# Query and key norms of a gated delta layer: the keys' read off a diagonal, the queries' summed in 32-column tiles

## The reference, cut to what matters

```python
q, k, v = split(silu(causal_conv(hidden @ w_qkv, conv_w)))       # heads of 128
qf = q * rsqrt(sum(q * q) + 1e-6) * 128 ** -0.5
kf = k * rsqrt(sum(k * k) + 1e-6)
def step(state, xs):                                             # over the tokens
    state = state * exp(g_t)
    delta = (v_t - k_t @ state) * b_t
    state = state + outer(k_t, delta)
    out = q_t @ state
```

## Time and profile before

| | |
|---|---|
| median of three runs | 1787.74 us (1787.28 to 1789.94) |
| the profiled execution | 1803.65 us, span 1802.1 us |
| TensorE matmuls | 1571.8 us busy, 87% of the span |
| VectorE | 1033.7 us, 57% |
| ScalarE | 771.8 us, 43% |
| GpSimd | 800.1 us, 44% |
| key and query norms (L593) | 512 passes, 60.5 us |
| k_root (L1056) | 16, mean 1638 ns |
| loads of A0, issue to landing | 2.6 us, median |

### The profile page before, as it was taken

One profiled execution on the slowest core, in us unless ns is written; L12 is line 12 of the kernel. 1 busy time (PEld: TensorE's weight loads), 2 busy tenths in 40 slices (PEclk: granted clock), 3 DMA queues, 4 the chain that ended last, 5 costly groups with the idle time before them and its releaser, 6 DMA issues. The chain is left out here.

```text
span 1802.1 us, 27445 instructions
## 1 busy us (share of the span) xinstructions
PE 1571.8 (87%) x9790; PEld 1149.2 (64%) x9790; DVE 1033.7 (57%) x2127; ACT 771.8 (43%) x1745; POOL 800.1 (44%) x1336
## 2 busy tenths in 40 slices
PE   3749999999999999999999999986979995978860
PEld 2436777777777777777778778764547764635540
DVE  4426677677777777777777777553035555312323
ACT  1325565565565565565565655541124331100110
POOL 0367667656656756757657657100000000061326
PEclk9779999999999999999999999998989996789995
DMA  4111111111111111111111111004210001023424
GB/s 154 38 27 26 32 38 28 36 33 30 39 33 30 34 33 36 33 33 36 34 33 37 33 33 23 8 10 197 112 30 1 1 1 53 1 85 86 144 86 116
DMA packets 119087, 84.41 MB, mean 47 GB/s; under 512 B 92658, under 2 KB 104518, under 8 KB 118192
## 3 DMA queue, kind: packets, MB, share of 16 engines
q1 hardware_dynamic: 112304, 64.73, 13.1%
q0 software_dynamic: 6656, 18.01, 3.3%
HBM read 63.00 MB, written 20.05 MB: 46 GB/s over the span
## 5 line engine op out<-in xcount | busy, mean ns | idle before, releaser
L580 PE MATMUL psum_banks<-main_hT,heads_w_in 128*128 128x512 f32 x512 | 248.7, 612 | 19.1 <-DVE heads_y L882 11.0
L882 DVE SCALAR_TENSOR_TENSOR heads_y<-psum_banks,gdn_conv_w,heads_y 128x1021 f32<-128x1021 f32 (+2 forms) x192 | 244.7, 1275 | 28.4 <-ACT heads_y L756 27.4
L1069 POOL TENSOR_TENSOR heads_XT<-heads_XT,heads_tmp 128x126 f32<-128x126 f32 (+22 forms) x496 | 207.1, 418 | 38.9
L1066 POOL TENSOR_TENSOR heads_tmp<-heads_XT,heads_A 128x126 f32<-128x126 f32 (+22 forms) x496 | 184.0, 371 | 38.9
L1604 POOL DMA_INDIRECT expert_rows<-moe_xn,route_dest x32 | 31.4, 981 | 365.5 <-issue 365.5
L580 PEld LDWEIGHTS psum_banks<-main_hT,heads_w_in 128*128 128x128 f32 x512 | 93.9, 196 | 94.8 <-issue 69.4
L667 PE MATMUL psum_banks<-heads_w_z,main_hT 128*128 128x256 f32 x512 | 126.6, 392 | 0.0
L693 PE MATMUL psum_banks<-heads_w_o,heads_ogT 128*128 128x256 f32 x512 | 119.2, 381 | 2.9 <-ACT heads_ogT L818 1.0
L756 ACT ACTIVATE heads_y<-psum_banks,gdn_conv_w 128x1024 f32<-128x1024 f32 x64 | 71.3, 1114 | 114.2 <-PE psum_banks L580 114.2
L778 ACT ACTIVATE heads_Dt<-heads_Dl,gdn_coef 128x128 f32<-128x128 f32 x224 | 77.4, 393 | 90.7 <-DVE heads_Dl L895 89.3
L1053 POOL TENSOR_TENSOR heads_Dm<-heads_Dm,main_upto 128x512 f32<-128x512 f32 x64 | 87.0, 1380 | 52.8 <-ACT heads_Dm L816 52.8
(11 more groups left out here) (249 smaller groups left out, 3511.0 us busy)
## 6 DMA issues: line engine op xcount, KB each, us to landing
main_w_gu<-in_w_gu SPq DMA_DIRECT2D x4, 2816.0 KB, 24.9
heads_w_in<-in_w_in SPq DMA_DIRECT2D x16, 512.0 KB
heads_A<-kk_blocks SPq DMA_DIRECT2D x64, 128.0 KB, 2.6
moe_wd<-in_w_down POOLq DMA_DIRECT2D x32, 176.0 KB, 2.7
expert_rows<-main_zeros SPq DMA_DIRECT2D x1, 4096.0 KB, 14.5
heads_w_z<-in_w_z SPq DMA_DIRECT2D x16, 256.0 KB, 2.7
heads_w_o<-in_w_o SPq DMA_DIRECT2D x16, 256.0 KB, 2.7
inverse_blocks<-heads_XT SPq DMA_DIRECT2D x32, 128.0 KB, 2.9
```

What stands on the lines that cost most here:

```text
L580: ins = pe.matmul(out[:, half * 512:(half + 1) * 512], w_in[:, kd_, j * P:(j + 1) * P], hT[:, kd_, half * 512:(half + 1) * 512], start=kd_ ...
L882: dve.scalar_tensor_tensor(y[j][:, shift:T], src[:, 0:T - shift], conv_w[:, head, j, t:t + 1], y[j][:, shift:T], ALU.mult, ALU.add).then_i ...
L1066: pool.tensor_tensor(tmp[:, 0:n, 0:m], bc_last(XT[:, 0:n, j], m), bc_mid(A0[:, j, j + 1:BLK], n), ALU.mult).then_inc(solve_step.sem, 1)
L1069: pool.tensor_tensor(XT[:, 0:n, j + 1:BLK], XT[:, 0:n, j + 1:BLK], tmp[:, 0:n, 0:m], ALU.add).then_inc(solve_step.sem, 1)
```

## The change

The products for the key norms, the squares of the keys and their PSUM bank's slot go. `block_scales` now also turns `nd`, which holds the squared norms (plus 1e-6) block by block, on VectorE in four squares of 32 x 32, and copies from it, quadrant by quadrant, to `k_norm`; GpSimd takes `k_root` inside `eliminate`, behind the scaling of A0. The query norms stay on TensorE, with the operands' places exchanged: the stationary operand is 32 columns of ones, and the squares are streamed, block b of all chunks (256 columns) to the partitions 32b to 32b+31. All 32 rows of such a block are equal, so VectorE turns the result from PSUM to `q_rows` and takes every 32nd column.

```diff
-    [("norm_k", 1), ("u6a", 3), ("u6b", 0)],
+    [("u6a", 3), ("u6b", 0)],
...
-AT = {"variance": 3, "factors": 6, "turn": 8, "scales": 13, "keys": 5, "key_squares": 8}
+AT = {"variance": 3, "factors": 6, "turn": 8, "scales": 13, "keys": 5}
...
+    q_rows = a.sb("q_rows", [P, C, BLK])
-    ones_col = a.sb("ones_col", [P, 1])
+    ones_col = a.sb("ones_col", [P, BLK])
+    nd_t = a.sb("nd_t", [P, BLK])
...
             def norms(out, squares):
-                for c in range(C):
-                    ins = pe.matmul(out[:, c:c + 1], squares[:, c * P:(c + 1) * P], ones_col[:], start=True, stop=True)
+                tokens = squares[:].rearrange("p (c b i) -> p b c i", b=NB, i=BLK)
+                for b in range(NB):
+                    ins = pe.matmul(out[BLK * b:BLK * (b + 1), 0:C * BLK], ones_col[:], tokens[:, b], start=True, stop=True)
                 return ins
...
-            pe.wait_ge(k_ready.sem, 2)
             pe.wait_ge(s_const, 1)
-            pe.wait_ge(s_first_kneg, 1)
-            norms(pair[:, 0:P], y[0]).then_inc(s_first_norm, 1)
...
-            key_squares(0, 1)
...
                 dve.tensor_tensor(cb[:], rnd[:], beta_rows[:, h], ALU.mult).then_inc(cb_step.sem, 1)
+                dve.transpose(nd_t[:], nd[:]).then_inc(cb_step.sem, 1)
+                dve.wait_ge(cb_step.sem, cb_step.done(h, "turned"))
+                wait(dve, k_root_ready, k_root_ready.base(h))
+                for b in range(NB):
+                    r = slice(BLK * b, BLK * (b + 1))
+                    dve.tensor_copy(k_norm[r], nd_t[r, b:BLK:NB]).then_inc(k_norm_ready.sem, 1)
...
                 elif name == "norm_q":
                     dve.wait_ge(full[b].sem, full[b].done(h, name))
+                    dve.transpose(flat(q_rows[:]), flat(bank[b][:])[:, 0:C * BLK]).then_inc(free[b].sem, 1)
+                    dve.wait_ge(free[b].sem, free[b].done(h, name))
                     wait(dve, q_root_ready, q_root_ready.base(h))
-                    dve.tensor_scalar(q_norm[:], bank[b][:, 0, 0:C], EPS, None, ALU.add).then_inc(free[b].sem, 1)
+                    dve.tensor_scalar(q_norm[:], q_rows[:, :, 0], EPS, None, ALU.add).then_inc(q_norm_ready.sem, 1)
...
                 if j == 1:
-                    dve.wait_ge(s_first_norm, 1)
-                    dve.tensor_scalar(k_norm[:], pair[:, 0:C], EPS, None, ALU.add).then_inc(s_first_sum, 1)
...
-            def key_root():
+            def key_root(h):
+                pool.wait_ge(k_norm_ready.sem, k_norm_ready.end(h))
                 pool.tensor_tensor(k_root[:], k_norm[:], powers[:, 0:C], ALU.pow).then_inc(k_root_ready.sem, 1)
...
             def eliminate(h):
                 pool.wait_ge(cb_step.sem, cb_step.done(h, "cb"))
                 pool.tensor_tensor(A0[:], A0[:], bc_mid(cb[:], BLK), ALU.mult).then_inc(solve_step.sem, 1)
+                key_root(h)
```

More of the change, by code:

```diff
@@ L247, in belongs @@
         return h in FINISH
-    if name.startswith("kk") or name.startswith("p") or name == "norm_k":
+    if name.startswith("kk") or name.startswith("p"):
         return h in AHEAD
@@ L496, in heads @@
     w_o_ready = per_head("w_o_loaded", "w", steps=FINISH)
-    k_ready = per_head("keys_ready", "k", "sk", before=2, steps=AHEAD)
+    k_ready = per_head("keys_ready", "k", before=1, steps=AHEAD)
     act_ready = per_head("silu_ready", "q", "sq", "v0", "v1")
-    k_root_ready = per_head("key_root_ready", "it", before=1, steps=AHEAD)
+    k_norm_ready = per_head("key_norm_ready", "0", "1", "2", "3")
+    k_root_ready = per_head("key_root_ready", "it")
+    q_norm_ready = per_head("query_norm_ready", "it")
     q_root_ready = per_head("query_root_ready", "it")
@@ L504, in heads @@
     blk_loaded = per_head("kk_blocks_loaded", "0", "1", "2", "3")
-    cb_step = per_head("block_scale_step", "nd", "rnd", "cb")
+    cb_step = per_head("block_scale_step", "nd", "rnd", "cb", "turned")
     solve_step = per_head("solve_step", "scale", "init", *[f"{o}{j}" for j in range(BLK - 1) for o in "ma"])
@@ L514, in heads @@
     s_const, s_own = a.sem("constants_ready"), a.sem("own_row_loaded")
-    s_first_kk, s_first_kneg, s_first_norm, s_first_sum = (a.sem(n) for n in ("first_kk", "first_kneg", "first_norm", "first_norm_read"))
+    s_first_kk, s_first_kneg = (a.sem(n) for n in ("first_kk", "first_kneg"))
     def flat(ap):
@@ L637, in product @@
                     pe.wait_ge(k_ready.sem, k_ready.done(h, "k"))
-                elif name == "norm_k":
-                    pe.wait_ge(k_ready.sem, k_ready.done(h, "sk"))
                 elif name == "norm_q":
@@ L674, in product @@
                 elif name.startswith("norm"):
-                    norms(bank[b][:, 0], y[int(name == "norm_q")]).then_inc(full[b].sem, 1)
+                    norms(flat(bank[b][:]), y[1]).then_inc(full[b].sem, 1)
                 elif name.startswith("k"):
@@ L760, in keys @@
                 act.activation(kT[h % 3][:], y[0][:], ACT.Silu).then_inc(k_ready.sem, 1)
-            def key_squares(h, before):
-                act.wait_ge(k_ready.sem, before)
-                act.activation(y[0][:], kT[h % 3][:], ACT.Square).then_inc(k_ready.sem, 1)
             def scan_quantum(h, c, part):
@@ L853, in activations @@
                         keys(h + 1, conv_done.done(h, "02"))
-                    if k == AT["key_squares"]:
-                        key_squares(h + 1, k_ready.done(h, "k"))
             for j in range(4):
@@ L963, in evacuate @@
                     dve.tensor_copy(flat(k_tok[par][:, 4 * u:4 * u + 4]), flat(bank[b][:])).then_inc(free[b].sem, 1)
[L964 to L967, removed]
                 elif name == "norm_q":
                     dve.wait_ge(full[b].sem, full[b].done(h, name))
+                    dve.transpose(flat(q_rows[:]), flat(bank[b][:])[:, 0:C * BLK]).then_inc(free[b].sem, 1)
+                    dve.wait_ge(free[b].sem, free[b].done(h, name))
                     wait(dve, q_root_ready, q_root_ready.base(h))
-                    dve.tensor_scalar(q_norm[:], bank[b][:, 0, 0:C], EPS, None, ALU.add).then_inc(free[b].sem, 1)
+                    dve.tensor_scalar(q_norm[:], q_rows[:, :, 0], EPS, None, ALU.add).then_inc(q_norm_ready.sem, 1)
                 elif name.startswith("v"):
                     if u == 0:
-                        dve.wait_ge(k_root_ready.sem, k_root_ready.base(h))
+                        dve.wait_ge(k_root_ready.sem, k_root_ready.end(h))
                     dve.wait_ge(full[b].sem, full[b].done(h, name))
@@ L1009, in _ @@
                     conv_tap(j, t, 0, first_pairs[j], j + 1, 3 * j + t)
-                if j == 1:
-                    dve.wait_ge(s_first_norm, 1)
-                    dve.tensor_scalar(k_norm[:], pair[:, 0:C], EPS, None, ALU.add).then_inc(s_first_sum, 1)
             block_scales(0)
@@ L1073, in _ @@
                 columns_of_g(0, g)
-            pool.wait_ge(s_first_sum, 1)
-            key_root()
             eliminate(0)
@@ L1078, in _ @@
                 if h in INVERT:
-                    b = BANK["norm_q"]
-                    pool.wait_ge(free[b].sem, free[b].done(h, "norm_q"))
+                    pool.wait_ge(q_norm_ready.sem, q_norm_ready.done(h, "it"))
                     pool.tensor_tensor(q_root[h % 2][:], q_norm[:], powers[:, C:2 * C], ALU.pow).then_inc(q_root_ready.sem, 1)
@@ L1090, in _ @@
                         columns_of_g(h + 1, g)
-                    b = BANK["norm_k"]
-                    pool.wait_ge(free[b].sem, free[b].done(h, "norm_k"))
-                    key_root()
                     b = BANK["u6a"]
```

1 line of the change is left out of this document (removed).

## The result

The changed kernel takes **1836.37 us** (median of four runs, 1834.31 to 1840.19); the kernel before, on the same chip, 1787.57 us (1787.28 to 1789.94). The ratio is 1.027, 95% interval 1.0252 to 1.0293: 2.7% slower, where +1.3% was forecast. The direction was right, the size wrong; the time lies 10 us above the range.

A forecast was written before the change was run, and what follows sets the result against it. The prediction took VectorE to pace TensorE around slot 4, despite TensorE's high busy share. Key part 21.0, query part 6.4, less 0.9, 1.0 and 1.4, made +24.1 us: 1811.8 us, range 1776 to 1826.

The forecast's parts named there:

- rival (c): Head loop: as forecast, plus one more low-clock TensorE stretch a step, +20 us, 1832 us; chance 0.10.
- (d): The forecast itself: copies held up, no added clock loss, +24.1 us, 1811.8 us; chance 0.57.
- query part, a step: Slot 4, VectorE: the PSUM transpose delays tap and X by 0.46 us a step (up to 1.7), steps 1 to 14.
- D, held up: Slot 13, VectorE: delay of the tap behind cb if the first copy waits for GpSimd's A0 product, 2.8 us.
- key part, a step: Slot 13: with the copies held up each step grows by 1.5 us, in steps 1 to 14.
- D, not held up: Slot 13, VectorE: the tap's delay by transpose, wait and four copies if unhindered, 0.46 to 0.8 us.
- key part then, a step: Slot 13: with unhindered copies each step gains 0.5 to 0.83 us.
- ahead of the loop and step 0: Without VectorE's wait for the first key norms: -1.0 us ahead of the loop, -1.4 us in step 0.
- step 15, queries: Step 15, slot 4: VectorE has no taps, so S is ready earlier for L600: -0.9 us once.
- a step changes by D - 1.29: Slot 13: the tap's delay D less 1.29 us of slack before L619, with -1.06 us as floor.
- Rival (a): Slot 13: copies not held up, -0.83 us a step, -8.9 us in all, 1779 us; gains below D = 1.1; chance 0.31.
- Rival (b): Whole loop: TensorE alone is the bound, so its saved time counts, -47 us, 1741 us; chance 0.02.

The follow-up runs named there:

- k_only: The changed kernel without its query part (query norms from one-column matmuls as before): 1830.12 us, ratio 1.023 to the kernel before.
- filler_1: The changed kernel plus one unread 128x512 TensorE product behind slot 14: 1833.33 us, ratio 1.0147 to the kernel before, on a chip with slower times.
- early_copies: The changed kernel with the nd transpose and four copies moved ahead of the reciprocal and cb: 1780.49 us, ratio 0.9957 to the kernel before.
- filler_2: The changed kernel plus two unread 128x512 TensorE products behind slot 14: 1829.68 us, ratio 1.0138 to the kernel before, on a chip with slower times.
- q_only: The kernel before with only the query-norm part of the change: 1797.09 us, ratio 1.005 to the kernel before.
- early_again: Repeat, in the last series, of the changed kernel with transpose and copies ahead of reciprocal and cb: 1794.60 us, ratio 0.9966 to the kernel before.
- pool_waits: The changed kernel, but GpSimd waits for the four copies before its product on A: 1781.35 us, ratio 0.9962 to the kernel before.
- early_q_late: `early_copies` with the query transpose behind X and GpSimd taking the tail's power ahead of q_root: 1791.55 us, ratio 0.9939; again 1790.12 us, 0.9948.
- early_q_back: `early_copies` with the query norms as in the kernel before: 1798.15 us, ratio 0.9975 to the kernel before; again 1788.78 us, 0.9933.
- after_again: The changed kernel, unaltered, run again in the last series: 1856.66 us, ratio 1.0306 to the kernel before.

## Why the prediction was right or wrong

**The step that failed** is the treatment of rival (c). The forecast (d) costs the clock at nothing, and (c), at +20 us and a chance of 0.10, was what happened. The fillers give the size: 22 to 23 us in the steps 2 to 14, 19.7 to 23.4 over the whole loop. The text had named both waits (1.3 and 1.9 us; 1.21 and 2.00 measured) and the price of a stretch, 1.46 us, and its range had room for two or three stretches; it gave no reason why a wait of 1.9 us in each step should leave the clock alone. The runs show that mostly it doesn't: 2.0 us of standing is followed by the low clock in eleven of twelve steady steps of the changed kernel and in all twelve of `k_only`, 0.94 to 1.2 us in none (`filler_1`, and slot 4 in `early_copies`).

**The rest of the sum held.** Without those falls (`filler_2`) the loop's last start lies 1240.62 - 1215.28 = 25.3 us behind the kernel before; +24.1 was forecast. In `filler_1` it is 29.0, most of the difference from ahead of the first slot-3 line. Term by term:

| term | forecast | measured |
|---|---|---|
| query part, a step | +0.46 us | +0.48 (`q_only`, 69.16 less 68.68) |
| D, held up | 2.8 | 3.14 (3.93 less 0.79) |
| key part, a step | +1.5 | +1.81 (`filler_2`, 70.97 less 69.16) |
| D, not held up | 0.46 to 0.8 | 0.94 (`early_copies`, 1.73 less 0.79) |
| key part then, a step | -0.5 to -0.83 | -0.34 (68.82 less 69.16) |
| ahead of the loop and step 0 | -2.4 | -2.7 (`filler_2`) and +0.1 (`filler_1`), at the first slot-3 line less one step's growth; open |
| step 15, queries | -0.9 | -0.7 (`q_only`, 58.79 against 59.51 us) |
| the three low stretches of the kernel before | not in the sum | -4.3 (gone in `filler_2` and `early_copies`; 1.43 us each) |

The start term can't be read closer than that: `early_copies` passes the first slot-3 line at 220.74 us in one trace and at 223.03 in the other (`early_again`). The rule "a step changes by D - 1.29" stands: 3.14 gives 1.85 against 1.81 measured, 0.94 gives -0.35 against -0.34. Both values of D were too small mainly by the same cause: a copy of 32 x 8 needs a slot of 0.185 us (0.74 for four), taken at 0.08 to 0.15. Slot 4 was right in each detail: TensorE gained nothing from norms of 0.64 us (taken at 0.55), as S came when it came, and the transpose took 0.44 us (0.42).

**The hold-up.** The first copy, which starts 0.01 us behind GpSimd's product of 2.35 us, takes up to 2.37, and the other three 0.16 each. The runs show that the product's presence, and nothing about the copies, makes the difference; why it does, they don't show. The Trainium skill ("SBUF — State Buffer", Who interferes with whom) states that whoever comes second to the shared port pair is blocked for the whole instruction. By that rule the copy ends with the product, and the trace agrees: both end at about 478.3 us.

**Rival (a)** was the price of the change without the hold-up: 1779 us against 1780.49 and 1781.35 measured, with D at 0.94 just under its turning point of 1.1. Its sum was right by luck: the steps gain less (-0.34 against -0.83), and vanished low stretches make up for it: the three above and, in that trace of `early_copies` alone, one in step 15 (55.87 us at a clock of 1.00; 59.51 at 0.94 before, 58.75 at 0.94 in `pool_waits`, 57.51 at 0.97 in `early_again`). **Rival (b)**, TensorE alone, is out: in `early_copies` its busy time falls by 2.45 us a step and the step grows by 0.14.

**The range** ended at 1826 because it left (c) outside. (c) stood at 1832, and even that was 4 us short: D was taken 0.34 us too small, which is 4.8 us over 14 steps.

What stays open: why a wait of 2.00 us left the clock alone in the changed kernel's first steady step, in both its traces, why some of the others have a mean clock of 0.98 and some of 0.95, and why the falls of the kernel before come in every fourth or fifth step and those of `q_only` in every second. No run was made for it.

## What to carry to other kernels

A small VectorE copy from SBUF to SBUF can cost what a GpSimd instruction beside it still has to run; put it ahead of the release of GpSimd's work, or let GpSimd wait for it (here 2.15 us a step at the full clock, 70.97 less 68.82, and 3.2 to 5.1 us where the clock fell too). When a change makes TensorE stand for 2 us where it was busy, price the clock with it: the lost stretch cost nearly as much as the wait. And read the clock of the old kernel too: behind work of few columns that looks busy it had low stretches, and their going gave back 4 us that no sum of durations contains.

## What the runs showed of the hardware that was not expected

- TensorE's clock fell to 1.2 GHz with TensorE busy all the time: behind 1.8 us of one-column products and 1.1 us of products on 32 x 32 tiles (`q_only`, 0.57 mean clock from 536.5 to 540.5 us). With the one-column key norms gone and no wait of 2 us, none of the steady steps of `early_copies`, `pool_waits` and `early_q_late` has such a stretch, though TensorE is busy for up to 2.5 us less in them than in the kernel before. `early_q_back`, which keeps the one-column query norms, has one in its two traces of twelve steady steps each, right behind those norms (mean clock 0.63 from 226.3 to 230.0 us).
- TensorE's clock fell behind 2.0 us of standing in 23 of 24 steady steps (the changed kernel and `k_only`), and behind 0.94 or 1.2 us in none. Filling that time with unread products of 1.9 us a step made the changed kernel faster: 1.0138 times the kernel before in place of 1.0272 (1.0306 on the chip of the last series).
- Eight passes of 256 columns into four column tiles of 32 take 0.64 us together.
- Between chips the head loop repeats to 0.1 us in the changed kernel (1037.65 and 1037.62 us from the first to the last slot-3 line) and to 2.1 us in `early_copies` (986.35 and 988.48, with one low stretch more), while the stretch behind it, which no kernel here changes, differs by up to 28 us (564 us in the profile of `q_only`, 592 in that of `after_again`). For a change inside the loop the windows of its steps tell more than the total.
